# The row maxima of both attentions: one transposition for four, and a VectorE multiplication that spreads them over the four slots of a bank

## What is computed

```python
x = x + attn(layernorm(x))            # 16 heads of 16, plus 4 latent heads over pooled tokens
x = x + xattn(layernorm(x), ctx)      # 16 heads of 16, then residual q and a layer norm
x = x + ffn(layernorm(x))             # 64 slots, top 8, a GRU step
# inside both attentions, per sequence and head:
scores = where(causal, q @ k.T / 4, NEG)
probs = softmax(scores)               # exp(scores - max over keys) / sum
out = probs @ v
```

## Time and profile before

| what | value |
|---|---|
| median of three runs | 1640.93 us (1639.8 to 1641.42) |
| the profiled execution, its own time | 1646.24 us |
| span of the profiled execution | 1644.5 us |
| mean granted TensorE clock | 0.967 of full speed |
| self attention, steady steps | two steps in 45.12 us |
| cross attention, steady steps | two steps in 33.82 us |
| TensorE / VectorE / ScalarE / GpSimd busy | 94% / 70% / 58% / 52% of the span |

### The profile page before, as it was taken

One profiled execution on the slowest core, in us unless ns is written; L12 is line 12 of the kernel. 1 busy time (PEld: TensorE's weight loads), 2 busy tenths in 40 slices (PEclk: granted clock), 3 DMA queues, 4 the chain that ended last, 5 costly groups with the idle time before them and its releaser, 6 DMA issues. The chain is left out here.

```text
span 1644.5 us, 52068 instructions
## 1 busy us (share of the span) xinstructions
PE 1538.9 (94%) x19038; PEld 1107.0 (67%) x19038; DVE 1155.0 (70%) x2897; ACT 959.7 (58%) x1926; POOL 859.9 (52%) x1178
## 2 busy tenths in 40 slices
PE   5999999999999999996999999999999958999997
PEld 4677776777777677764677777777777635666664
DVE  5667777677777677762576767667676737998986
ACT  2555555555555555543666675766667516777773
POOL 2454444554444544433376666667666643555553
PEclk7999999999999999996999999999999968999998
DMA  5300000000000000002100000000000000000001
GB/s 158 117 2 1 0 0 0 0 0 0 0 0 0 0 0 0 1 2 84 42 15 20 13 13 19 13 19 13 19 13 13 3 0 7 33 32 32 32 32 39
DMA packets 31202, 32.31 MB, mean 20 GB/s; under 512 B 3937, under 2 KB 29602, under 8 KB 31138
## 3 DMA queue, kind: packets, MB, share of 16 engines
q1 hardware_dynamic: 31138, 31.46, 6.2%
HBM read 23.06 MB, written 8.39 MB: 19 GB/s over the span
## 5 line engine op out<-in xcount | busy, mean ns | idle before, releaser
L1455 DVE TENSOR_REDUCE c_neg_max<-score_banks 128x16 f32<-128x2048 f32 x64 | 146.6, 2290 | 98.5 <-PE score_banks L1229 98.5
L998 POOL TENSOR_TENSOR a_less<-a_attn,a_remote 128x512 f32<-128x512 f32 x32 | 40.7, 1273 | 265.2 <-DVE a_attn L846 265.2
L984 POOL TENSOR_SCALAR_AFFINE_SELECT a_probs_t<-a_probs_t 128x512 f32<-128x512 f32 x256 | 158.0, 647 | 33.5 <-ACT a_probs_t L669 33.4
L669 ACT ACTIVATE a_probs_t<-score_banks 128x512 f32<-128x512 f32 x256 | 135.7, 601 | 48.6 <-PE score_banks L513 48.6
L826 DVE TENSOR_REDUCE a_neg_max<-score_banks 128x16 f32<-128x2048 f32 x64 | 146.4, 2288 | 21.0 <-PE score_banks L481 21.0
L1564 POOL TENSOR_SCALAR_AFFINE_SELECT c_probs_t<-c_probs_t 128x512 f32<-128x512 f32 x256 | 154.8, 639 | 9.7 <-ACT c_probs_t L1383 9.7
L1383 ACT ACTIVATE c_probs_t<-score_banks 128x512 f32<-128x512 f32 x256 | 132.3, 602 | 17.5 <-PE score_banks L1257 15.8
L361 PE MATMUL side_banks<-a_xn_t,a_w_qk 128*128 128x256 f32 x512 | 133.9, 396 | 1.3 <-ACT a_xn_t L613 1.3
L361 PEld LDWEIGHTS side_banks<-a_xn_t,a_w_qk 128*128 128x128 f32 x512 | 92.9, 196 | 11.1 <-ACT a_xn_t L613 1.7
L1575 POOL TENSOR_TENSOR c_scaled<-c_normed,gamma 128x512 f32<-128x512 f32 x32 | 40.6, 1268 | 97.7 <-DVE c_normed L1438 97.7
L1836 PE MATMUL side_banks<-w_ih,gi_t 128*128 128x512 f32 (+1 forms) x256 | 88.3, 487 | 0.4 <-DVE n_in L2002 0.2
(11 more groups left out here) (254 smaller groups left out, 4192.1 us busy)
## 6 DMA issues: line engine op xcount, KB each, us to landing
x_sb<-in_x SPq DMA_DIRECT2D x32, 256.0 KB, 2.9
c_ctx_in<-in_ctx SPq DMA_DIRECT2D x32, 256.0 KB, 2.7
out<-y SPq DMA_DIRECT2D x32, 256.0 KB, 2.1
w_ih<-in_ffn_w_ih SPq DMA_DIRECT2D x1, 768.0 KB, 6.8
w_hh<-in_ffn_w_hh SPq DMA_DIRECT2D x1, 768.0 KB, 7.7
a_raw_qk<-in_attn_qk_w SPq DMA_DIRECT2D x1, 512.0 KB, 3.5
a_raw_cross<-in_xattn_qk_w SPq DMA_DIRECT2D x1, 512.0 KB, 4.4
b_ih<-in_ffn_b_ih SPq DMA_DIRECT2D x1, 384.0 KB, 6.2
```

The costliest lines, as they stand in the source:

```text
L669: nc.scalar.activation(probs_t[tt][:, 4 * g:4 * g + 4, :].rearrange("p j q -> p (j q)"), score_banks[:, g, :], ACT.Exp, scale=SCALE).then_ ...
L984: nc.gpsimd.affine_select(out=probs, in_=probs, pattern=[[0, 4], [1, 128]], compare_op=ALU.is_ge, fill=0.0, base=-1, channel_multiplier=-1 ...
L1455: nc.vector.tensor_reduce(neg_max[:, tt, :], all_scores, AX.X, ALU.max, negate=True).then_inc(max_done, 1)
```

## The change

It changes how `max_t` is made, in both attentions, and the order of the work around it.

- `max_part` becomes one 128x128 matrix per sequence: column 32i + 2j + u holds part u of the maximum of bank i and slot j.
- `max_transpose` is one transposition instead of four.
- ScalarE's `copy_max` goes. In its place VectorE's `spread_max` multiplies the transposed 128x128 result, read four times from PSUM, with a constant `row_slot` (128x4 of 0 and 1 in fp32), and writes the 128x512 `max_t`.
- On VectorE, spread_max(prev, 0) stands after row_max(prev, 1) and before max_parts(prev, 1); spread_max(prev, 1) stands after normalise(old, 1) (and gate_logits).
- On TensorE, max_transpose(prev, 1) moves to just behind scores_t(prev, 0). In the self attention project_q(at, 1) now comes ahead of project_lat(at), which waits for both spreads of the pair before instead of the first copy; the three waits on evac_lat move from max_transpose to lat_values.
- `row_slot` is reduced once from the identity at the start; the initial zeroing of `max_part` is a quarter as long.

```diff
-    max_part = sb("max_part", [128, 2, 4, 128], BF16)
+    max_part = sb("max_part", [128, 2, 128], BF16)
...
             def project_lat(at):
                 pe.wait_ge(pooled_ready, at.count(1, 1))
-                wait(pe, maxT_ready, at.count(2, -1))
+                wait(pe, maxT_ready, at.count(2, 0))
...
                 pe.wait_ge(maxT_ready, at.count(2, 2))
+                if more(at):
+                    pe.wait_ge(rq_ready, at.count(1, 2))
+                    pe.wait_ge(rk_ready, at.count(1, 2))
+                    pe.wait_ge(rv_ready, at.count(1, 2))
...
-                for j in range(4):
-                    mm = pe.transpose(maxT_bank[:].bitcast(BF16)[:, 128 * j:128 * j + 128], max_part[:, tt, j, :],
-                                      ident_bf[:])
-                mm.then_inc(maxT_filled, 1)
+                pe.transpose(maxT_bank[:].bitcast(BF16)[:, 0:128], max_part[:, tt, :], ident_bf[:]).then_inc(maxT_filled, 1)
...
                 if prev.real:
                     scores_t(prev, 0)
+                if prev.real:
+                    max_transpose(prev, 1)
                 if at.real:
+                    project_q(at, 1)
                     project_lat(at)
-                    project_q(at, 1)
                 if prev.real:
                     lat_transpose(prev)
-                    max_transpose(prev, 1)
...
-            def copy_max(at, tt):
-                act.wait_ge(maxT_filled, at.count(2, tt + 1))
-                wait(act, sct_filled, at.count(2, tt - 1))
-                nc.scalar.activation(max_t[:, tt, :], maxT_bank[:].bitcast(BF16)[:, 0:512],
-                                     ACT.Copy).then_inc(maxT_ready, 1)
...
-                parts = max_part[:, tt, :, :].rearrange("p j (i u) -> p u i j", i=4)
+                parts = max_part[:, tt, :].rearrange("p (i r) -> p i r", i=4)[:, :, 0:8].rearrange("p i (j u) -> p u i j", u=2)
...
+            def spread_max(at, tt):
+                dve.wait_ge(maxT_filled, at.count(2, tt + 1))
+                wait(dve, sct_filled, at.count(2, tt - 1))
+                nc.vector.tensor_tensor(max_t[:, tt, :].rearrange("p (j q) -> p j q", j=4),
+                                        maxT_bank[:].bitcast(BF16)[:, 0:128].unsqueeze(1).to_broadcast([128, 4, 128]),
+                                        cross.row_slot[:].unsqueeze(2).to_broadcast([128, 4, 128]),
+                                        ALU.mult).then_inc(maxT_ready, 1)
...
                     row_max(prev, 1)
+                    spread_max(prev, 0)
                     max_parts(prev, 1)
                 if old.real:
                     normalise(old, 1)
                     gate_logits(old)
+                if prev.real:
+                    spread_max(prev, 1)
                 if at.real:
                     evac_lat(at)
...
+            slots = ident[:].rearrange("p (i r) -> p i r", i=4)[:, :, 0:8].rearrange("p i (j u) -> p j i u", u=2)
+            nc.vector.tensor_reduce(cross.row_slot[:], slots, AX.XY, ALU.add).then_inc(rows_made, 1)
```

More of the change, by code:

```diff
@@ L166, in __init__ @@
         self.row_half = sb("row_half", [128, 2])
+        self.row_slot = sb("row_slot", [128, 4])
         self.b_k = sb("b_k_half", [128, 2, 2])
@@ L489, in max_transpose @@
                     wait(pe, av_ready, at.count(2, 0))
-                elif more(at):
-                    pe.wait_ge(rq_ready, at.count(1, 2))
-                    pe.wait_ge(rk_ready, at.count(1, 2))
-                    pe.wait_ge(rv_ready, at.count(1, 2))
                 else:
                     pe.wait_ge(maxT_ready, at.count(2, 1))
-                for j in range(4):
-                    mm = pe.transpose(maxT_bank[:].bitcast(BF16)[:, 128 * j:128 * j + 128], max_part[:, tt, j, :],
-                                      ident_bf[:])
-                mm.then_inc(maxT_filled, 1)
+                pe.transpose(maxT_bank[:].bitcast(BF16)[:, 0:128], max_part[:, tt, :], ident_bf[:]).then_inc(maxT_filled, 1)
             def scores_t(at, tt):
@@ L701, in step @@
                     copy_remote(old)
-                if prev.real:
-                    copy_max(prev, 0)
                 if at.real:
@@ L710, in step @@
                     gate_tanh(old)
-                if prev.real:
-                    copy_max(prev, 1)
                 if at.real:
```

4 lines of the change are left out of this document (2 added, 2 removed).

## The result

The changed kernel took **1652.85 us** (median of 4 executions, 1652.14 to 1654.06) against 1640.37 us for the kernel before (4 executions, 1639.76 to 1641.42). The ratio is 1.0077, 95% interval [1.0064, 1.0089]: slower by some 12.5 us. The forecast was 1642.3 and its range ended at 1652. The profiled execution of the changed kernel took 1652.47 us for a span of 1650.7.

A forecast was written before the change was run, and what follows sets the result against it. The prediction took TensorE to be the bound, with VectorE's two reductions setting self-attention time up to scores_t(prev, 0). Self +5.6 and cross -4.2 gave +1.4 us on the median 1640.93: 1642.3 us, range 1633 to 1652.

The forecast's parts named there:

- Transpositions before scores_t(prev, 0), saving 0: Both attentions: TensorE arrives 0.15 us earlier but waits that much longer for VectorE's two reductions, so nothing is saved.
- Second transposition, self, 0.15 a step: Self attention, TensorE: one transposition instead of four, moved behind scores_t(prev, 0) without waiting, gains 0.15 us per step.
- Length of the spread, 0.69 and 0.61: VectorE's spread_max: 0.69 us long, 0.61 from its start to the next instruction's, taken from a similar PSUM operation.
- Stall before project_lat, 0.28 and 0.37, mean 0.32: Self attention: TensorE waits at project_lat for the second spread, 0.28 us in one step and 0.37 in the other.
- Net of the self attention, +5.6 us: Self attention: stall less the transposition's 0.15 us saving, mean 0.175 us over 32 steps, 5.6 us slower.
- The moved transposition costs 0.08 before project_q: Cross attention, TensorE: max_transpose(prev, 1) ahead of project_q adds only its own 0.08 us.
- Gain of the moved transposition, 0.13 a step: Cross attention: scores_t(prev, 1) starts earlier, gain cut to 0.13 us by the fourth exponential, 4.2 us over 32 steps.
- the exponentials take all of it: Cross attention: lower bound of the moved transposition's gain, 0 us, against at most 0.15 us per step.
- Idle time of VectorE as the cover of two spreads (1.22 in 1.55 us): Cross attention, VectorE: two spreads fill 1.22 us of the 1.55 us idle before the bias of v.
- The slower rival: VectorE's second spread holds TensorE longer: 1649 us, or 1653 if exponentials also take the cross attention's gain; chance 0.35.
- The sum itself: Whole kernel: 5.6 - 4.2 = +1.4 us on the median 1640.93; a 0.66 us spread estimate would add 1.6 us.
- the forecast's case: Self attention stall of 0.2 to 0.38 us with the cross attention's gain: 1637.6 to 1644.2 us, chance 0.37.

The follow-up runs named there:

- the one with the old place: Changed kernel with max_transpose(prev, 1) of the cross attention back behind project_v(at, 0): 1648.81 us, 1.0041 to the kernel before.
- the last combined kernel: Changed kernel with first spreads on ScalarE, self attention's lat_norm between gate_logits and second spread, lat_transpose ahead of project_lat: 1642.22 us, 1.0008 to the kernel before.

## Why the prediction was wrong, point by point

- **Transpositions before scores_t(prev, 0), saving 0:** right. TensorE arrived earlier and waited longer (0.16 and 0.44 us in the two steps shown), and the norm moved later showed the chain that eats it.
- **Second transposition, self, 0.15 a step:** right. A single one takes 0.07 start to start (310.44 to 310.51), and alone, in the kernel before, it was worth 0.17 a step.
- **Length of the spread, 0.69 and 0.61:** right, 0.68 and 0.60.
- **Stall before project_lat, 0.28 and 0.37, mean 0.32:** 0.29 in both steps (331.86's step: project_q at 333.25, project_lat at 334.45, less 0.91). The small difference that I took over from the second step didn't stay.
- **Net of the self attention, +5.6 us:** the mechanism right, the size over, at 16 x 0.09 = 1.4. Apart from the 0.03 of the stall, the step won 0.04 up to scores_t and 0.05 at the project_v behind lat_transpose (1.02 instead of 1.07 from start to start); both lie in terms that I had at 0. Why project_v is shorter there wasn't tested; with lat_transpose ahead of project_lat it takes 1.07 again. max_parts itself is shorter with the new layout (0.18 and 0.18 against 0.20 and 0.23 us).
- **Cross attention, "The moved transposition costs 0.08 before project_q": the step that failed.** The sum has no wait there and takes max_parts, for which the transposition waits, as fast as before. The 0.5 to 0.6 us that the first spread adds ahead of max_parts were priced in the self attention and found hidden by 0.4 us. In the cross attention I didn't redo the working, and never set GpSimd's timeline beside it: the spread there puts max_parts under an addition that holds it for another 1.1 us. TensorE's wait of 0.61 and 0.44 us in the two steps shown took the place of the gain, and two steps take 0.60 us more where 0.26 less was forecast. The trace of before had the sign of it, in rows that the prediction didn't use: at the same place the copy L1462 took 0.43 us instead of 0.20 and ended 0.05 after GpSimd's L1578, the operation ahead of the addition. Timelines of the kernel before, GpSimd and VectorE:

```profile
1010.41 1.27 POOL L1578 TENSOR_TENSOR c_shifted<-c_scaled,beta 128x512 f32<-128x512 f32 x1
...
1011.30 0.43 DVE L1462 CAST c_max_part<-c_neg_max 128x16 bf16<-128x16 f32 x1
```

- **Gain of the moved transposition, 0.13 a step:** wrong too, it is 0 to 0.03. The lower bound that I named, "the exponentials take all of it", is the case, as the time of 1.36 us from the fourth exponential to the next projection shows in both kernels. I let the matmuls of the fourth bank run on unhindered once released; in the kernels measured, moving scores_t(prev, 1) ahead of the exponentials' end was waited off. Alone in the kernel before, the shorter transpositions gave the cross attention 0.05 per two steps.
- **Idle time of VectorE as the cover of two spreads (1.22 in 1.55 us):** right for the spreads, too small for what they brought with them. Without GpSimd's addition the same spreads cost nothing (33.85 against 33.82), and VectorE still idles 27.2 us in 28 steps before the bias of v, of 47.7 in the kernel before. The hold of 1.1 us comes on top: the changed kernel keeps 7.7 us, and the one with the old place has none in the step shown and loses 0.43 per two steps.
- **The slower rival** had the right sign and about the right size (1649 to 1653) but named the second spread in the self attention; what came was the first spread, in the cross attention.
- **The sum itself:** it comes out, but for two small things. The range of the forecast's case begins at 1638.4, not 1637.6, for a stall of 0.2; and a spread longer by 0.05 us would count twice before project_lat, 3.2 us and not 1.6. Neither bears on the result.

By the measured terms: 1.4 + 9.6 = 11.0 us on 1640.9 give 1651.9, against 1652.85.

## What to carry to other kernels

When an instruction is put ahead of others on VectorE, price everything behind it at its new time, and set GpSimd's timeline beside it: a small instruction that slides under a long GpSimd operation can cost that operation's remainder, not its own length (here 1.28 us for 0.18). An engine's idle time covers added work only if it also covers what that work is pushed into, and a saving ahead of a wait on another engine (here four exponentials, or two reductions) is worth nothing until that other chain gets shorter. Work is best moved to where the receiving engine waits just then: the first spread is longer on ScalarE than on VectorE, and moving it there took the kernel from 1652.85 to 1637.44 us.

## What was not expected of the hardware

- The hold lasts to the very end of GpSimd's operation (within 0.04 us in all 30 cases of the changed kernel's addition) and doesn't go by size: 1.28 us for 128x16 with both inputs in SBUF and 1.10 for a 128x16 copy with its one input there, 0.68 for 128x512 with one input in PSUM and one in SBUF. GpSimd's own time stays 1.27 us.
- Some of an instruction's own length passes under the hold. L1454 started 1.25 us before the addition's end and lost 1.10 (1.28 - 0.18). a_lat_w, 128x512, started 0.53 us before the end of a GpSimd subtraction in the last combined kernel, took 1.08 us instead of 0.75 and lost 0.33; it ended 0.55 after the subtraction, as it did in 31 of 32 cases.
- The passage between the attentions, from the last latent evacuation of the self attention (a_rq_f) to the first bias of v in the cross attention, is 64.7 us long in the profile before and 59.9 in the one after, with the granted clock of these rows, a mean between its two levels. The windows of the kernel before (us, then busy time of PE, PEld, DVE, ACT and POOL, the granted clock, DMA share and GB/s):

```profile
745.00:785.00 40.00, 26.66 (x168) 19.77 (x172) 11.58 (x35) 12.07 (x23) 9.69 (x14) 0.65 0.33 107
```

The same windows of the changed kernel:

```profile
745.00:785.00 40.00, 25.05 (x180) 18.31 (x180) 13.52 (x36) 12.70 (x25) 10.86 (x15) 0.79 0.35 114
```

It isn't the change: the kernel before with one transposition alone has 59.9 us there, and the kernel before without the addition 64.7. These 4.8 us are about what the profile before lies above its median (5.3), and they are why the periods are the better measure here than the two spans, whose difference (1650.7 - 1644.5 = 6.2) hides half of the loss. What sets the length of the passage stays open.
